# Softmax probabilities of a cross-attention: split into halves before the transpose, and transposed by DMA instead of by TensorE

## The reference

```python
def _L0_xattn_ref(x, context, ln_gamma, ln_beta, w_q, w_kv, w_out, b_out, gate):
    xn = _layernorm(x, ln_gamma, ln_beta)
    q = (xn @ w_q).reshape(B, SQ, 16, 64)
    k, v = jnp.split(context @ w_kv, 2, axis=-1)      # k, v to (B, 375, 16, 64)
    scores = jnp.einsum('bqhd,bkhd->bhqk', q * SCALE, k)
    attn = jax.nn.softmax(scores, axis=-1)
    out = jnp.einsum('bhqk,bkhd->bqhd', attn, v).reshape(B, SQ, 1024)
    return (out @ w_out + b_out) * jnp.tanh(gate[0])

x = _layernorm(x + self_attention(x))
x = _layernorm(x + _L0_xattn_ref(x, ctx_1024, ...))
x = _layernorm(x + moe_ffn(x))
```

## Time and profile before

| | |
|---|---|
| median of 3 runs | 754.85 us (753.52 to 756.06) |
| profiled execution, its time | 755.73 us |
| its span | 753.9 us |
| PE | 615.0 us busy, 82% |
| PE's weight loads | 483.4 us, 64% |
| DVE | 480.8 us, 64% |
| ACT | 402.7 us, 53% |
| POOL | 265.2 us, 35% |

### The profile page before, as it was taken

The page is one execution under the profiler, slowest core; times in us unless marked ns, Lnnn a source line. Parts: engine busy times, 40 slices in busy tenths (PEclk is TensorE's granted clock), DMA queues, the critical chain, the costliest instruction groups (busy, mean ns, idle before and its releaser), DMA issues. The chain is left out here.

```text
span 753.9 us, 14298 instructions
## 1 busy us (share of the span) xinstructions
PE 615.0 (82%) x4746; PEld 483.4 (64%) x4746; DVE 480.8 (64%) x903; ACT 402.7 (53%) x989; POOL 265.2 (35%) x290
## 2 busy tenths in 40 slices
PE   4735778989999999999999999999669737899990
PEld 3524657877877877777777778777455533466660
DVE  3894336777777877776777777766649544843332
ACT  2444137567567567576577576465425414844431
POOL 3451013254254343343343353343413701133331
PEclk9965569999999999999999999999778977999995
DMA  8625110110110210210110200400324741633324
GB/s 226 210 86 175 20 47 29 42 48 28 49 37 28 60 52 28 50 44 28 48 47 28 59 36 28 124 29 29 112 98 166 248 144 47 194 62 59 58 31 109
DMA packets 58645, 57.34 MB, mean 76 GB/s; under 512 B 17266, under 2 KB 47986, under 8 KB 58610
## 3 DMA queue, kind: packets, MB, share of 16 engines
q1 hardware_dynamic: 54514, 51.68, 22.5%
q0 software_dynamic: 4096, 5.19, 4.2%
HBM read 46.74 MB, written 10.13 MB: 75 GB/s over the span
## 5 line engine op out<-in xcount | busy, mean ns | idle before, releaser
L631 POOL TENSOR_TENSOR c_rcp<-c_sum,neg_one 112x2 f32<-112x2 f32 x64 | 44.6, 697 | 217.2 <-ACT probs L768 217.2
L635 POOL TENSOR_TENSOR probs<-probs,c_rcp 112x750 f32<-112x750 f32 x64 | 92.0, 1437 | 5.0
L768 ACT ACTIVATE probs<-ps_s,c_neg 112x375 f32<-112x375 f32 x128 | 72.7, 581 | 22.6 <-DVE c_neg L993 22.0
L666 ACT ACTIVATE kt_hi<-ps_o 128x376 fp32r<-128x376 f32 x64 | 31.9, 498 | 76.4 <-PE ps_o L145 76.4
L1618 POOL DMA_INDIRECT moe_sum<-gsh_hi,xs_in x21 | 33.4, 1589 | 102.6 <-ACT gsh_hi L1669 69.2
L988 DVE SCALAR_TENSOR_TENSOR v_lo<-ps_vx,v_scale,v_hi 125x512 f16<-125x512 f32 x48 | 35.9, 749 | 47.0 <-ACT v_hi L760 47.0
L997 DVE SCALAR_TENSOR_TENSOR cpt_lo<-ps_t,cpt_hi 125x672 f16<-125x672 f32 x64 | 54.4, 850 | 12.5 <-ACT cpt_hi L775 12.5
L1310 PE MATMUL ps_t<-ident,probs 112*125 112x112 f32 x384 | 53.8, 277 | 8.7 <-DVE cpt_lo L997 8.6
L993 DVE TENSOR_REDUCE c_neg<-ps_s 112x2 f32<-112x750 f32 x64 | 59.5, 929 | 1.9 <-PE ps_s L145 1.7
L1938 PE MATMUL ps_h<-w_ex,xst_hi 128*128 (+1 forms) x168 | 58.5, 390 | 1.0 <-DVE xst_lo L1705 0.9
L1310 PEld LDWEIGHTS ps_t<-ident,probs 112*125 112x125 f32 x384 | 49.9, 193 | 12.6 <-POOL probs L635 7.6
(11 more groups left out here) (307 smaller groups left out, 1845.3 us busy)
## 6 DMA issues: line engine op xcount, KB each, us to landing
chunk<-in_L_ffn_ew_dram SPq DMA_DIRECT2D x24, 512.0 KB, 3.5
spare<-in_L_ffn_ew_dram SPq DMA_DIRECT2D x18, 512.0 KB, 5.2
store<-in_L_ffn_ew_dram SPq DMA_DIRECT2D x6, 512.0 KB, 5.5
ctx_all<-in_ctx_dram SPq DMA_DIRECT2D x2, 1500.0 KB
ctx_raw<-in_ctx_dram SPq DMA_DIRECT2D x8, 375.0 KB
moe_in<-chunk SPq DMA_DIRECT2D x1, 2709.0 KB, 14.0
xs_in<-moe_in SPq DMA_DIRECT2D x21, 129.0 KB, 2.1
plain_raw<-in_L_xattn_w_kv_dram SPq DMA_DIRECT2D x2, 1024.0 KB, 15.9
```

Of the source, the lines that this page charges most:

```text
L631: pool.tensor_tensor(c_rcp[:, s % 2, :], c_sum[:, s % 2, :], neg_one[:, :], ALU.pow).then_inc(sg["c_rcp_ready"], 1)
L635: pool.tensor_tensor(p, p, r, ALU.mult).then_inc(sg["p_normed"], 1)
L768: act.activation(probs[:, s % 2, h, :], ps_s[0:N, h, 0:SK], ACT.Exp, bias=c_neg[:, s % 2, h:h + 1], accum_out=c_sum[:, s % 2, h:h + 1]).th ...
```

## The change

- DVE and ACT now split the probabilities where they lie, with the queries in the partitions. POOL makes the reciprocal and multiplies it (112x2) with 2^14, and the product of the 112x750 goes. ACT writes the high part as `probs` times `c_rcp` into an fp16 tensor `p16` (two instructions of 112x375, `p_hi`, at the end of step s for pair s), DVE the low part into the same tensor (two instructions, `p_lo`, in step s+1 after the maxima, in every step).
- SP transposes `p16` of a pair, both heads and both parts, by one DMA (`transpose_p`): 112 rows of 1536 fp16 into 128 x 12 x 112. PE's `p_transpose` and the bank `ps_t` go. The keys stand in pieces of 128, 128 and 119 instead of three of 125, with zeros up to 384.
- `k_project` has a bank of its own, `ps_kt`, in place of `ps_t`. Its wait for `oct_lo` goes, and `pv`'s for `kt_lo`.
- `exps` of pair s waits for `p_lo` of pair s-2 instead of its transpose. `pv` waits for the DMA.
- SP's queue is written out anew, step by step, with one transpose ahead of each step's other transfers. In an entry that has a next one the chunks come after the transposes of pairs 1, 2 and 6, the `o_shuffle` store after the second of these, the `o_rows` load after the transpose of pair 3, and `ctx_raw` and `x_res` (for the entry after the next) after that of pair 4. In the last entry a chunk follows each of the transposes of pairs 2 to 6.

The diff, cut to its core:

```diff
-        cpt = half_pair(nc, ctx, "cpt", [SKT, 2, ST, N])
+        p16 = sb("p16", [N, 2, 2, 2, PW], F16)
+        p_scale = sb("p_scale", [N, 2])
+        p16_t = sb("p16_t", [P, 2, 4 * ST, N], F16)
...
-        ps_t = ctx.enter_context(nc.psum_tensor("ps_t", [P, 2, 512], F32))
+        ps_kt = ctx.enter_context(nc.psum_tensor("ps_kt", [P, 512], F32))
...
-        ps_k = ps_o[:, 0:SKP]
+        ps_k = ps_kt[:, 0:SKP]
...
+            def transpose_p(b, s):
+
+                n = PAIRS * b + s
+                sp.wait_ge(sg["p_lo"], n + 1)
+                if later(n - 1):
+                    sp.wait_ge(sg["pv_full"], n - 1)
+                sp.dma_start_transpose(p16_t[:, s % 2, :, :], p16[:, s % 2, :, :, :].rearrange("p a h n -> p (a h n)"))\
+                    .then_inc(sg[f"p_t{s % 2}"], 16)
...
             for b in range(B):
-                entry(b)
-
-            sp.wait_ge(sg["qk_hi"], 4 * B)
-            sp.wait_ge(sg["qk_lo"], 3 * B)
-            sp.wait_ge(sg["k_lo"], B)
-            sp.dma_start(gw_raw[:, :, :], A["gate_w"].rearrange("(k p) e -> p k e", p=P)).then_inc(ffn_sg["gw_loaded"], 16)
-            load_weights(sp, raw, A["sw1"], A["sw2"], A["sw3"], ffn_sg["raw_loaded0"])
-            for q in range(3 * (B - 1), CHUNKS):
-                load_chunk(q)
+                more = b + 1 < B
+                for s in range(PAIRS):
+                    transpose_p(b, s)
+                    if not more and s == 0:
+                        load_ffn()
+                    if more and s == 1:
+                        load_chunk(3 * b + 1)
+                    if more and s == 2:
+                        load_chunk(3 * b + 2)
+                        store_o(b + 1)
+                    if more and s == 3:
+                        load_o(b + 1)
+                    if b + 2 < B and s == 4:
+                        load_ctx(b + 2)
+                        load_x(b + 2)
+                    if more and s == 6:
+                        load_chunk(3 * b + 3)
+                    if not more and 2 <= s < 7:
+                        load_chunk(3 * b + s - 1)
...
             def normalise(b, s):
                 pool.wait_ge(sg["c_exp"], 2 * (PAIRS * b + s) + 2)
-                pool.tensor_tensor(c_rcp[:, s % 2, :], c_sum[:, s % 2, :], neg_one[:, :], ALU.pow).then_inc(sg["c_rcp_ready"], 1)
+                if later(PAIRS * b + s - 1):
+                    pool.wait_ge(sg["p_lo"], PAIRS * b + s - 1)
+                pool.tensor_tensor(c_rcp[:, s % 2, :], c_sum[:, s % 2, :], neg_one[:, :], ALU.pow).then_inc(sg["c_rcp_part"], 1)
+                pool.wait_ge(sg["c_rcp_part"], PAIRS * b + s + 1)
+                pool.tensor_tensor(c_rcp[:, s % 2, :], c_rcp[:, s % 2, :], p_scale[:, :], ALU.mult).then_inc(sg["c_rcp_ready"], 1)
                 pool.wait_ge(sg["c_rcp_ready"], PAIRS * b + s + 1)
-                p = probs[:, s % 2]
-                r = c_rcp[:, s % 2].unsqueeze(2).to_broadcast([N, 2, SK])
-                pool.tensor_tensor(p, p, r, ALU.mult).then_inc(sg["p_normed"], 1)
...
                 if later(PAIRS * b + s - 1):
-                    act.wait_ge(sg["t_full"], PAIRS * b + s - 1)
+                    act.wait_ge(sg["p_lo"], PAIRS * b + s - 1)
...
+            def p_hi(b, s):
+                act.wait_ge(sg["c_rcp_ready"], PAIRS * b + s + 1)
+                n = PAIRS * b + s
+                if later(n - 1):
+                    act.wait_ge(sg[f"p_t{s % 2}"], 16 * (PAIRS // 2 * b + s // 2))
+                for h in range(2):
+                    last = act.activation(p16[:, s % 2, 0, h, 0:SK], probs[:, s % 2, h, :], ACT.Copy, scale=c_rcp[:, s % 2, h:h + 1])
+                last.then_inc(sg["p_normed"], 1)
...
-                    if s >= 1:
-                        cpt_hi(b, s - 1)
-                    elif later(b):
-                        cpt_hi(b - 1, 7)
+                    p_hi(b, s)
...
+            def p_lo(b, s):
+                dve.wait_ge(sg["p_normed"], PAIRS * b + s + 1)
+                for h in range(2):
+                    last = dve.scalar_tensor_tensor(p16[:, s % 2, 1, h, 0:SK], probs[:, s % 2, h, :], c_rcp[:, s % 2, h:h + 1],
+                                                    p16[:, s % 2, 0, h, 0:SK], op0=ALU.mult, op1=ALU.subtract)
+                last.then_inc(sg["p_lo"], 1)
...
-            def pv(b, s, k_done):
-                pe.wait_ge(sg["cpt_lo"], PAIRS * b + s + 1)
+            def pv(b, s):
+                pe.wait_ge(sg[f"p_t{s % 2}"], 16 * (PAIRS // 2 * b + s // 2 + 1))
                 pe.wait_ge(sg["v_lo"], v_no("V02" if s < 4 else "V12", b))
-
-                pe.wait_ge(sg["kt_lo"], k_done)
```

105 lines of the change are left out of this document (45 added, 60 removed).

## The result

The changed kernel takes 772.88 us (median of 4 runs, 770.78 to 773.75) against 754.18 for the kernel before; the ratio is 1.0244, with a 95% interval of 1.0209 to 1.028. The forecast was 773.2 and slower, with a range of 735 to 825. The profiled execution took 772.29 us, its span is 770.5.

The account below looks back on a forecast made before the run. Middle entries bound by waits for ACT and DVE rather than TensorE, the last by chunk loads. 755.73 + 1.4 (middle) + 18.0 (last) - 1.0 (tail) = 774.1, less 0.9 to the median: 773.2; range 735 to 825, own 764 to 788.

Parts of the forecast that it names:

- the ring: Last entry: maxima, p_lo, transpose, chunk and chunk_max wait on each other in a circle, 8.67 us per step, +18.0 us.
- the tail: From the last chunk_max to the last product with V: -1.0 us, with about 1 us for slower matmuls included.
- The transposing DMA: Each pair's transpose takes 3.5 us (range 2.8 to 14), hidden in entries 0 to 6.
- Rival (b): The transposing DMA is slow, 8 us, in middle and last entries: 820 us; chance 0.17.
- TensorE: Removing six transposes per step gains only in steps 0 and 4, 0.75 us each, 1.5 per entry.
- the last sentence of the prediction: It would be wrong if ACT's waits for GpSimd exceeded 0.3 per step, or the lower clock came into middle entries.
- The middle entries together: 1.5 us gained, 0.8 lost through ACT and DVE, 0.5 through the load; reckoned +0.2 per entry, +1.4 for seven.
- The own bank: A separate bank for ps_k drops waits on oct_lo and kt_lo; counted within the 1.5 us of steps 0 and 4.
- ACT and DVE: ACT +0.3 us and DVE +0.2 per step; steps 0, 2 and 5 affected, 0.8 per middle entry lost.
- SyncE's queue: Middle entries: the o_rows load lands later behind a chunk and a transpose, PE waits 0.2 to 1.2 us, 0.5 taken.
- Rival (a): TensorE is the path after all, 41.5 us come off the middle entries: 730 us, faster; chance 0.13.
- rival (c): The last entry's circle does not close, since chunks loaded alone come much sooner than 4.0 us: about 755; chance 0.08.

Follow-up runs that it names:

- e1: The changed kernel with each chunk load of the last entry one transpose earlier in SyncE's queue: 751.08 us, ratio 0.9955 to the kernel before.
- e2: The kernel before, with each last-entry chunk load after the first also waiting for cpt_lo of the next step: 763.45 us, ratio 1.012.
- e3: The changed kernel with six idle transposes on PE per step, where the old ones stood: 772.84 us, ratio 1.0245 to the kernel before.
- e4: The kernel before with one of the six PE transposes of each step left, the first pair excepted: 756.87 us, ratio 1.0004.
- e8: e1 with the keys' product back in the output bank and its old waits: 775.1 us, five runs 773.66 to 778.71 and one 755.29.
- e6: e1 with p_lo of step 5 moved behind ot_lo on DVE: 751.36 us, ratio 0.9946 to the kernel before.
- e5: e1 with idle PE transposes put only where PE waited, 28 per entry: 748.66 us, ratio 0.9912 to the kernel before.
- e9: e1 with the order of e6, the idle work of e5, and the o_shuffle store and o_rows load ahead of the third chunk: 744.41 us, ratio 0.9856.

## Why the prediction was right, point by point

The total came within 0.3 us, and that is partly luck. The largest term, the ring, was right in mechanism and size. But inside the ring two terms were wrong in opposite directions, and in the middle entries a gain that had not been forecast was taken back by a clock that had not been forecast.

**The last entry: +18.0 - 1.0 forecast, +17.3 measured.** The mechanism is the one described: e1 takes it away (-19.1) and e2 makes it in the kernel before (+6.5 of 7.4). Its terms were off in ways that cancelled. The issue of a transpose holds SP's queue for 1.42 us until the chunk's issue, not 0.37; from its issue to its reading a chunk took 3.8, 4.1, 4.2, 5.4 and 4.4 us in the five rings, so the delay by the rows of the transpose, taken at 1.0, was 0.4 in the mean and 1.4 in the fourth. `p_lo` took 1.12 for 1.05. The rings are 8.3, 8.7, 8.8, 9.8 and 8.9 us, 8.67 forecast. From the last `w_max` to the FFN it is 11.07 us after and 12.00 before: -0.9, with -1.0 forecast, and the first three steps of the entry gave 1.0 more, which had not been forecast. The part of the tail that had no row, about 1 us for slower matmuls, cannot be taken out of the -0.9; the matmuls of the last product take 0.31 us for the 0.24 of the earlier trace rows.

**The transposing DMA: 3.5 taken, 3.5 measured** (3.4 to 7.2 over all 64). The nearest rows, the store (2.8) and the chunk (3.9), were the right guides. The reading of the earlier trace rows was a little off: the store fills four slices, 1.2 us, and not five. The transposes raised the DMA share of the middle entries by 1.7 us of all 16 engines for each, more than the 1.3 to 1.5 that were read from the store. By the figure of the Trainium skill in "VectorE: DVE Perf Modes", § The three transpose paths, 1309 ns for a 128x128 piece, an estimate that adds up the pieces is 13.7; in this trace the 10.5 pieces of one DMA land after 3.5 together, so they do not add up in that way. Rival (b) needed 8 us.

**TensorE: 1.5 per entry forecast; 1.1 per entry at a clock of 0.97 by e3, 0.4 for five sixths of the transposes by e4.** That most of the 6 us per entry only lengthen waits is shown by these two runs and by the list of PE's waits, whose partners are those forecast (`qt_lo`, `ot_lo`, `pt_lo`, `xn`, `res`, the exps). The step that failed was to take the clock as granted alike in all middle entries, before and after. It came in as the last sentence of the prediction says.

**The middle entries together: +0.2 each forecast, -0.2 each measured (336.86 to 335.75 us in six).** The small number is luck. At like clock an entry is 1.4 us shorter, not 0.2 longer: 8.4 in six entries, and five more low stretches at about 1.5 took 7.3 back. The gain is in step 0 (6.16 to 5.16 us), which was forecast at nothing, and in the steps 3 and 4 (15.4 to 13.7 together where they hold one low stretch); the loss is in step 5 (6.88 to 7.82), with 0.2 and 0.3 in the steps 1 and 2. With PE's load put back (e3) step 0 takes 5.70, so about half of its gain is PE's; with five sixths of PE's load taken from the kernel before (e4) it stays at 6.16, so that half needs the rest of the change as well. What gave the other half is not shown.

**The own bank.** It was read as nothing of its own. By e8 it is about 1.2 us per entry, 0.6 of it read directly: a mis-sized term. It is one of the reasons why the entries came out shorter at like clock.

**ACT and DVE.** `p_hi` takes 1.11 for the pair where 1.05 was taken, and `p_lo` 1.12. ACT waited for GpSimd 1.0 us in the six entries together, and GpSimd's second multiply takes 0.20, near the lower bound. That `p_lo` ahead of `ot_lo` in step 5 costs 0.75 is not borne out: e6 moved it away and the step lost 0.2. In step 0 one of the 16 instructions of `p_lo` in an entry took 1.14 us instead of 0.60, while `stack_lo` ran on GpSimd, 0.5 of the 0.7 allowed, and off the path. By the Trainium skill, "SBUF — State Buffer", § SBUF: two separate sides, a VectorE operation with two inputs in SBUF and a GpSimd operation that reads SBUF do not share the pair of ports between them: whichever starts first has it for its whole instruction. The row agrees, with 0.5 us more.

**SyncE's queue.** 0.5 us per entry had been charged for the `o_rows` load. In the changed kernel PE's weight loads waited for it twice, 0.7 us together in six entries. In e1 PE waited 2.8 us in three entries, and with the clock kept up 6.7 in five (e5). So the term was too large here; the low stretch ahead of the load seems to cover it, and e9, where the load is earlier and the wait is gone, fits that.

Rival (a), PE as the bound, falls by e3 and e4. Rival (b) falls by the landing at 3.5 us, rival (c), that the ring would not close, by the five rings in the trace.
